# Where the SyncE queue issues the reload of the fourth expert's split weights

## The chip, the cores and the metric

One core of one Trainium2 chip runs the kernel. The metric is the device time of one launch in microseconds (us); where several runs are given, the median counts. Engines: TensorE (PE) multiplies matrices, VectorE (DVE), ScalarE (ACT) and GpSimd (POOL) do the rest, and SyncE (SP) issues most DMA transfers. "POOLq", "SPq" and so on are the instruction queues of these engines.

## The reference

The kernel computes a gated cross-attention layer and then a mixture of experts, on 32 sequences of 128 tokens of 256 values (4096 tokens).

```
x = x + tanh(g_xattn) * attention(layernorm(x), ctx, ctx)     # 16 heads of 16, causal
xf = layernorm(x)
logits = xf @ Wr + br                                          # 8 experts
keep the two largest, softmax over them -> weights
h = gelu(einsum('td,edh->eth', xf, W1) + b1)                   # 256 -> 1024, exact gelu
y = einsum('eth,ehd->etd', h, W2) + b2                         # 1024 -> 256
x = x + tanh(g_ffn) * sum over the kept experts of y * weights
```

## The kernel before

The program has two blocks, one after the other, each with its own instruction stream for every engine, and a barrier of all engines between them.

**The attention block** (`attention_and_routing`) runs a software pipeline over 16 groups of two sequences. Beside the attention it does three things for the experts. It splits each expert's W1 and W2 into a high and a low float16 part and stores them in DRAM (`split_weights`, `w_dram`), one layer of one expert with each group. It routes: for each token and each of its two experts POOL writes the token's normalised row into that expert's region of `token_rows` (`xs_dram`) with an indirect DMA (L471). And at its end (`padding`, L49) SP and ACT each write four blocks of padding rows behind the eight regions.

The on-chip tensor `wts` holds the split weights of all eight experts, 2 MB for each, but the attention block uses the places of experts 4 to 7 for its own operands. Hence the weights are loaded back from DRAM by `load_weights` (L56), two DMAs of 1 MB each for an expert. Experts 0, 1 and 2 are reloaded in the last groups of the attention's loop, expert 3 (`EARLY - 1`) after the padding, and experts 4 to 7 in the experts' block. Below, w3 is the reload of expert 3, w4 that of expert 4, and so on. Before each reload SP waits until the one before it has landed (`weights_in`), and SP's instructions behind such a wait have to wait with it.

**The block's end.** SP waits for its last stores, POOL for its last indirect DMAs, and then every engine goes through the barrier (L308; POOL's part of it begins with a DRAIN instruction). PE has no work there.

**The experts' block** (`experts`) runs over 39 tiles of 256 token rows, sorted by expert. For tile i, SP loads the rows `xs` (L1120, 272 KB), eight buffers deep; PE transposes them (L1276), multiplies by W1 (L1292) and by W2 (L1308); ACT applies gelu; DVE splits into two float16 parts; ACT scales by the routing weight; POOL adds the result to the output with an indirect DMA (L1168). Iteration `it(i)` of SP loads the rows of tile i + 2, and in its first iterations also the second layer's bias (`b2_all`, 1 MB) and weights: in `it(-1)` the bias and w4, in `it(0)` w5, in `it(1)` w6 and w7. On PE, `it(i)` transposes tile i + 2 first, then does layer 1 of tile i + 1, then layer 2 of tile i, strictly in this order, so PE stands still in `it(i)` until the rows of tile i + 2 have landed. Below, "row load j" is the load of tile j's rows, tiles counted from 0.

SP's queue is one queue in program order. The last lines of the attention block on it:

```python
                loop_over_groups(sp, it)
                padding(sp, env, range(E // 2))
                sp.wait_ge(weights_in, 16 * 2 * (EARLY - 1))
                load_weights(sp, wts, w_dram, EARLY - 1, weights_in)
```

The functions in full:

Of the kernel before, what the change touches and what calls it, by code (L numbers as in the profile page):

```python
# [19 lines left out]
E = 8  # L20
# [17 lines left out]
EARLY = 4  # L38
# [5 lines left out]
def padding(eng, env, experts):  # L44

    eng.wait_ge(env["pad_rows_ready"], 1)
    for e in experts:
        place = eng.value_load(env["padplace"][0:1, e:e + 1], min_val=0, max_val=E * REG)
        eng.dma_start(env["xs_dram"][bass.ds(place, TILE), :].rearrange("(h p) r -> p h r", h=2),  # L49
                      env["padrow"][:, :].unsqueeze(1).to_broadcast([P, 2, ROW])).then_inc(env["pads_in"], 16)  # L50


def load_weights(sp, wts, w_dram, e, done):

    for layer in range(2):
        sp.dma_start(wts[:, e, 4096 * layer:4096 * (layer + 1)], w_dram[e, layer]).then_inc(done, 16)  # L56
# [27 lines left out]
def there(g):  # L84

    return 0 <= g < NG if isinstance(g, int) else True
# [75 lines left out]
def attention_and_routing(nc, env):  # L162
# [11 lines left out]
    with ExitStack() as stack:  # L174
# [133 lines left out]
        with nc.Block() as block:  # L308

            @block.sync  # L310
            def _(sp):
# [85 lines left out]

                loop_over_groups(sp, it)
                padding(sp, env, range(E // 2))
                sp.wait_ge(weights_in, 16 * 2 * (EARLY - 1))  # L400
                load_weights(sp, wts, w_dram, EARLY - 1, weights_in)
                for i in range(2):
                    arrived(sp, x2_stored, NG - 2 + i, i)
                    settled(sp)
# [619 lines left out]
def experts(nc, env):  # L1024
# [8 lines left out]
    with ExitStack() as stack:  # L1033
# [30 lines left out]
        def settled(eng):  # L1064

            eng.sem_inc(waits_taken, 1)
# [15 lines left out]
        def all_tiles(eng, it):  # L1082


            pipeline(eng, it, 0, MAIN_TILES)
            ties = eng.value_load(mostint[0:1, 0:1], min_val=0, max_val=E)
            with eng.If(ties > 2):
                pipeline(eng, it, MAIN_TILES, ALL_TILES)

        def when(eng, ok, s, value):  # L1090

            if ok:
                eng.wait_ge(s, value)

        def before(i, n):

            return i >= n if isinstance(i, int) else True
# [4 lines left out]
        def added_value(i):  # L1102

            return i * 16 + 16

        with nc.Block() as block:

            @block.sync
            def _(sp):
                sp.wait_ge(rows_placed, 1)  # L1110
                sp.wait_ge(pads_in, 16 * E)

                def it(i, m, there):
                    if there(2):

                        j = i + 2
                        when(sp, before(j, RING), added[1], added_value(j - RING))
                        settled(sp)
                        row = sp.value_load(tile_row[0:1, bass.ds(j, 1)], min_val=0, max_val=E * REG)
                        sp.dma_start(xs[(m + 2) % RING][:, :, :],  # L1120
                                     xs_dram[bass.ds(row, TILE), :].rearrange("(h p) r -> p h r", h=2)
                                     ).then_inc(row_in[(m + 2) % RING], 16)
                    if isinstance(i, int) and i == -1:
                        sp.dma_start(b2_all[:, :, :].rearrange("p e d -> p (e d)"), b2.partition_broadcast(P)).then_inc(b2_in, 16)
                    if isinstance(i, int) and -1 <= i <= 1:

                        for e in {-1: (EARLY,), 0: (EARLY + 1,), 1: range(EARLY + 2, E)}[i]:
                            sp.wait_ge(weights_in, 16 * 2 * e)
                            load_weights(sp, wts, w_dram, e, weights_in)

                all_tiles(sp, it)
                sp.wait_ge(weights_in, 16 * 2 * E)
                sp.wait_ge(b2_in, 16)
# [221 lines left out]
```

## Time and profile before

| | us |
|---|---|
| median of three runs | 1036.77 |
| the three runs | 1031.41, 1036.77, 1039.24 |
| the profiled execution, whole | 1034.72 |
| its span, first to last instruction | 1033.0 |
| TensorE busy (matmul) in the span | 917.5 |
| TensorE's mean granted clock | 0.876 |

All rows of the trace count in us from the span's start. The profiled execution took 1.7 us more than its span. A clock of 1.0 is TensorE's upper level (2.4 GHz), 0.5 the lower (1.2 GHz).

### The profile page before, as it was taken

The page shows a single profiled execution, that of the slowest core. Times are in us where ns is not written, and L with a number is a line of the kernel's source. Part 1 is how long each engine was busy: PE and PEld are TensorE (multiplying, and loading weights), DVE is VectorE, ACT ScalarE, POOL GpSimd, SP SyncE. Part 2 cuts the span into 40 slices and gives each one's busy share as a digit, 9 for nine tenths or more (in the row PEclk, how much of TensorE's full clock was granted, in tenths as well). Part 3 has the DMA queues.
Part 4 walks back from the last instruction along what each step waited for, and adds up shares of the span by engine and source line. Part 5 has one row for each costly group of instructions (what it writes and reads, how often), then busy time and mean ns, then how long its engine had stood idle before and what let it go on. Part 6 is the DMA issues. An engine that isn't in the chain of part 4 may idle for free. (4 is left out here: it accounts for less than half of the span.)

```text
span 1033.0 us, 25346 instructions
## 1 busy us (share of the span) xinstructions
PE 917.5 (89%) x7545; PEld 814.6 (79%) x7601; DVE 628.4 (61%) x1521; ACT 444.1 (43%) x962; POOL 345.0 (33%) x355
## 2 busy tenths in 40 slices
PE   3799999999999999999951989999989989999991
PEld 2688888888888888888941879889879978989881
DVE  3467778777777787777453645565536554555650
ACT  2454444554444554344310544544535444544530
POOL 2222455433454533444321022323312331332222
PEclk9888888888888988887555999999989999999996
DMA  8855666656667566666258743323323332332221
GB/s 161 152 99 160 179 175 166 149 131 178 175 174 179 128 148 171 175 159 206 98 211 314 291 122 48 56 48 49 60 39 49 48 55 32 60 47 46 27 27 24
DMA packets 86072, 124.34 MB, mean 120 GB/s; under 512 B 8928, under 2 KB 77664, under 8 KB 81760
## 3 DMA queue, kind: packets, MB, share of 16 engines
q1 hardware_dynamic: 70592, 102.90, 37.7%
q0 software_dynamic: 14304, 19.15, 12.0%
q8 instruction: 57, 0.93, 0.4%
q10 hardware_dynamic: 1088, 1.11, 0.3%
q14 instruction: 31, 0.25, 0.1%
HBM read 55.21 MB, written 42.75 MB: 95 GB/s over the span
## 5 line engine op out<-in xcount | busy, mean ns | idle before, releaser
L1168 POOL DMA_INDIRECT out_rows<-yg,xs x78 | 126.1, 1617 | 352.4 <-ACT yg L1210 208.8
L1292 PE MATMUL bank<-xh,wts 128*128 128x256 f16 x1872 | 217.4, 278 | 0.0
L1308 PE MATMUL bank<-wts,hh 128*128 x1872 | 210.6, 273 | 0.0
L1292 PEld LDWEIGHTS bank<-xh,wts 128*128 x1872 | 186.6, 100 | 24.2
L1308 PEld LDWEIGHTS bank<-wts,hh 128*128 128x128 f16 x1872 | 183.2, 98 | 21.2
L454 POOL TENSOR_SCALAR_AFFINE_SELECT probs<-probs 128x512 f32<-128x512 f32 x128 | 95.8, 749 | 276.7 <-ACT probs L519 276.3
L1200 ACT ACTIVATE hf<-bank,b1t,gscale 128x256 f32<-128x256 f32 x312 | 154.8, 562 | 25.6 <-PE bank L1292 23.4
L909 PE MATMUL bank<-va,probs 128*128 128x17 f32 x1024 | 149.9, 281 | 9.9 <-DVE ao L631 9.8
L909 PEld LDWEIGHTS bank<-va,probs 128*128 128x128 f32 x1024 | 143.3, 216 | 14.5 <-DVE ao L631 12.2
L519 ACT ACTIVATE probs<-bank 128x512 f32<-128x512 f32 x128 | 76.4, 597 | 149.5 <-PE bank L894 148.4
L1210 ACT ACTIVATE yg<-yb,xs 128x256 f32<-128x256 f32 x78 | 35.4, 500 | 204.2 <-DVE yb L1249 188.2
L1239 DVE SCALAR_TENSOR_TENSOR hh<-hf,hscale,hh 128x512 f16<-128x512 f32 x156 | 117.3, 752 | 5.6
L681 DVE TENSOR_REDUCE rowmax<-bank 128x4 bf16<-128x512 f32 x128 | 87.8, 686 | 32.8 <-PE bank L833 20.4
L1249 DVE SCALAR_TENSOR_TENSOR yb<-bank,yscale,b_all 128x512 f32<-128x512 f32 x39 | 29.3, 751 | 107.4 <-PE bank L1308 107.4
L1238 DVE TENSOR_SCALAR hh<-hf,hscale 128x512 f16<-128x512 f32 x156 | 75.8, 486 | 26.6 <-ACT hf L1200 26.2
L471 POOL DMA_INDIRECT token_rows<-pay,slots x64 | 71.4, 1115 | 21.7 <-issue 11.1
L1223 DVE SCALAR_TENSOR_TENSOR xh<-bank,xh 128x512 f16<-128x512 f32 x39 | 27.0, 691 | 82.5 <-ACT xh L1191 82.5
L833 PEld LDWEIGHTS bank<-wts 96*128 96x128 bf16 x512 | 44.9, 108 | 23.2 <-issue 9.0
L833 PE MATMUL bank<-wts 96*128 96x128 bf16 x512 | 57.5, 242 | 5.6 <-issue 3.2
L891 PE MATMUL bank<-negident,rowmax 128*128 128x128 bf16 x512 | 55.8, 237 | 4.3 <-DVE rowmax L681 4.2
L1276 PE MATMUL bank<-ident,xs 128*128 128x128 f32 x156 | 25.5, 289 | 34.4 <-DMA xs<-token_rows 25.1
L894 PE MATMUL bank<-wts 96*128 96x128 bf16 x512 | 55.4, 236 | 0.0
(165 smaller groups left out, 1206.3 us busy)
## 6 DMA issues: line engine op xcount, KB each, us to landing
wts<-in_W SPq DMA_DIRECT2D x16, 1024.0 KB, 7.4
split_weights<-wts SPq DMA_DIRECT2D x16, 1024.0 KB, 4.9
wts<-split_weights SPq DMA_DIRECT2D x16, 1024.0 KB, 8.1
wts<-keys SPq DMA_DIRECT2D x96, 128.0 KB, 3.9
wts<-queries SPq DMA_DIRECT2D x96, 128.0 KB
xs<-token_rows SPq DMA_DIRECT2D x39, 272.0 KB, 2.8
xin<-in_x SPq DMA_DIRECT2D x16, 256.0 KB, 4.9
cin<-in_ctx_in SPq DMA_DIRECT2D x16, 256.0 KB, 6.1
```

Of the source, the lines that this page charges most:

```text
L454: pool.affine_select(out=probs[q % 4][:, :, :], in_=probs[q % 4][:, :, :], compare_op=ALU.is_ge, fill=0.0, base=0, pattern=[[0, 4], [1, P] ...
L471: pool.indirect_dma_start(out=xs_dram[:, :], out_offset=bass.IndirectOffsetOnAxis(ap=slots[par][:, b, r:r + 1], axis=0), in_=pay[par][:, b ...
L519: act.activation(probs[q % 4][:, :, :].rearrange("p a q -> p (a q)"), TB[q % 2][:, :], ACT.Exp, scale=float(DK) ** -0.5).then_inc(exp_read ...
L681: dve.tensor_reduce(rowmax[n % 2][:, :], SB[n % 2][:, :].rearrange("p (a k) -> p a k", a=4), AX, ALU.max).then_inc(max_ready, 1)
L833: last = pe.matmul(ps[:, i * P:(i + 1) * P], qst[par][:, 2 * j + odd, tok], kst[par][:, 2 * j + odd, tok], start=False, stop=i == 3)
L909: last = pe.matmul(OB[:, h * VA:(h + 1) * VA], probs[m % 4][:, a, :], va[i][:, b, h, :], start=True, stop=True)
L1168: pool.indirect_dma_start(out=out[:, :], out_offset=bass.IndirectOffsetOnAxis(ap=numbers, axis=0), in_=yg[m % 2][:, half, :], in_offset=No ...
L1200: last = act.activation(hf[:, c, :], HB[quarter][:, c % 2 * TILE:(c % 2 + 1) * TILE], ACT.Gelu, bias=b1t[:, bass.ds(e, 1), c], scale=gscal ...
L1238: step(dve.tensor_scalar(high, full, hscale[:, bass.ds(e, 1)], None, ALU.mult))
L1239: dve.scalar_tensor_tensor(out=hh[b][:, 1, c, :].rearrange("p c t -> p (c t)"), in0=full, scalar=hscale[:, bass.ds(e, 1)], in1=high, op0=A ...
L1292: last = pe.matmul(HB[c // 2][:, c % 2 * TILE:(c % 2 + 1) * TILE], wts[:, bass.ds(expert[1], 1), at:at + P], xh[b][:, xp, k, :], start=q = ...
L1308: last = pe.matmul(YB[b][:, half * D:(half + 1) * D], hh[b][:, hp, c, half * P:(half + 1) * P], wts[:, bass.ds(expert[0], 1), at:at + D], ...
```

## The change

w3 is no longer issued at the end of the attention block but in `it(-1)` of the experts' block, behind row loads 0 and 1 and the bias, where w4 was. w4 moves to `it(0)`, together with w5. w6 and w7 stay in `it(1)`. The waits on `weights_in` move with the loads. No transfer is added or left out.

```diff
--- before.py
+++ after.py
@@ -397,8 +397,6 @@
 
                 loop_over_groups(sp, it)
                 padding(sp, env, range(E // 2))
-                sp.wait_ge(weights_in, 16 * 2 * (EARLY - 1))
-                load_weights(sp, wts, w_dram, EARLY - 1, weights_in)
                 for i in range(2):
                     arrived(sp, x2_stored, NG - 2 + i, i)
                     settled(sp)
@@ -1124,7 +1122,7 @@
                         sp.dma_start(b2_all[:, :, :].rearrange("p e d -> p (e d)"), b2.partition_broadcast(P)).then_inc(b2_in, 16)
                     if isinstance(i, int) and -1 <= i <= 1:
 
-                        for e in {-1: (EARLY,), 0: (EARLY + 1,), 1: range(EARLY + 2, E)}[i]:
+                        for e in {-1: (EARLY - 1,), 0: (EARLY, EARLY + 1), 1: range(EARLY + 2, E)}[i]:
                             sp.wait_ge(weights_in, 16 * 2 * e)
                             load_weights(sp, wts, w_dram, e, weights_in)
```

On SP, the end of the attention block and the start of the experts' block, as one piece of the difference (`wts<-split_weights` is a weight load, `tile_row` the register load of a tile's address, `xs0` the buffer of row load 0):

```order
 L49 ISA
 L49 DMA token_rows<-padrow 128x2x272
-L56 DMA wts<-split_weights 128x4096 [waits weights_in]
-L56 DMA wts<-split_weights 128x4096
 L308 UNCONDITIONAL_BRANCH [waits x2_stored0,w_stored0,x2_stored1,w_stored1,params]
-L1108 UNCONDITIONAL_BRANCH [waits barrier_Pool_Activation_PE_DVE_SP_release]
-L1119 TENSOR_LOAD tile_row [waits rows_placed,pads_in]
```

The two DMAs of w3 are gone between the last padding and the block's end; the rows from L1108 on stand in the changed kernel too, with line numbers lower by two.

On SP in the experts' block, from row load 2 on, the kernel before (the first pair is w5, the second w6, the third w7):

```order
L1120 DMA xs2<-token_rows 128x2x272
L56 DMA wts<-split_weights 128x4096 [waits weights_in]
L56 DMA wts<-split_weights 128x4096
L1119 TENSOR_LOAD tile_row
L1119 ISA x2
L1120 ISA
L1120 DMA xs3<-token_rows 128x2x272
L56 DMA wts<-split_weights 128x4096 [waits weights_in]
L56 DMA wts<-split_weights 128x4096
L56 DMA wts<-split_weights 128x4096 [waits weights_in]
L56 DMA wts<-split_weights 128x4096
```

One pair of weight DMAs, with one wait, stood between row loads 2 and 3. The same stretch of the changed kernel (the pairs are w4, w5 and w6):

```order
L1118 DMA xs2<-token_rows 128x2x272
L56 DMA wts<-split_weights 128x4096 [waits weights_in]
L56 DMA wts<-split_weights 128x4096
L56 DMA wts<-split_weights 128x4096 [waits weights_in]
L56 DMA wts<-split_weights 128x4096
L1117 TENSOR_LOAD tile_row
L1117 ISA x2
L1118 ISA
L1118 DMA xs3<-token_rows 128x2x272
L56 DMA wts<-split_weights 128x4096 [waits weights_in]
L56 DMA wts<-split_weights 128x4096
```

Two pairs with two waits now stand between row loads 2 and 3. In front of row load 2 there is one pair in both kernels, and between row loads 3 and 4 two pairs in both.

## Rows read from the trace of the kernel before

**Rows 1.** The page: the span, and TensorE's granted clock in 40 slices

```profile
span 1033.0 us, 25346 instructions
...
PEclk9888888888888988887555999999989999999996
```

**Rows 2.** Timeline of SP's queue, 500 to 620: start, duration, line, operation, count

```profile
541.55 5.52 SPq L49 DMA_DIRECT2D token_rows<-padrow  x4
547.11 2.48 SPq L56 DMA_DIRECT2D wts<-split_weights  x2
560.10 1.63 SPq L1120 DMA_DIRECT2D xs<-token_rows  x2
...
562.28 0.91 SPq L56 DMA_DIRECT2D wts<-split_weights  x2
563.98 0.39 SPq L1120 DMA_DIRECT2D xs<-token_rows  x1
573.18 0.80 SPq L56 DMA_DIRECT2D wts<-split_weights  x2
574.79 0.39 SPq L1120 DMA_DIRECT2D xs<-token_rows  x1
580.40 9.41 SPq L56 DMA_DIRECT2D wts<-split_weights  x4
590.73 21.74 SPq L1120 DMA_DIRECT2D xs<-token_rows  x6
```

**Rows 3.** Timeline of PE, 545 to 620; in brackets the idle time before and its releaser

```profile
562.87 1.11 PE L1276 MATMUL bank<-ident,xs 128*128 128x128 f32 x4 [21.23 <-DMA xs<-token_rows]
...
573.90 0.66 PE L1276 MATMUL bank<-ident,xs 128*128 128x128 f32 x4 [0.92 <-DMA xs<-token_rows]
...
584.88 0.60 PE L1276 MATMUL bank<-ident,xs 128*128 128x128 f32 x4
...
590.55 5.40 PE L1308 MATMUL bank<-wts,hh 128*128 x48
598.92 0.66 PE L1276 MATMUL bank<-ident,xs 128*128 128x128 f32 x4 [2.96 <-DMA xs<-token_rows]
599.41 7.07 PE L1292 MATMUL bank<-xh,wts 128*128 128x256 f16 x48
```

**Rows 4.** Line L308, the barrier: count, duration min/median/max in ns, first and last start

```profile
L308 SPq DRAIN  x1: 13/13/13, 550.1 to 550.1; - x1
L308 POOLq DRAIN  x1: 5295/5295/5295, 552.8 to 552.8; - x1
```

**Rows 5.** Line L1106, the barrier at the kernel's end

```profile
L1106 POOLq DRAIN  x1: 4095/4095/4095, 1028.6 to 1028.6; - x1
```

**Rows 6.** Landing times of w3's two DMAs (issued at 547.1 and 548.5)

```profile
DMA to landing us min/median/max: 8.7/9.2/9.7
```

**Rows 7.** Packets of all DMA queues, 549 to 551, then 553 to 555

```profile
DMA packets 519, 0.71 MB, mean 354 GB/s; under 512 B 58, under 2 KB 456, under 8 KB 519
...
DMA packets 115, 0.86 MB, mean 428 GB/s; under 512 B 8, under 2 KB 11, under 8 KB 11
```

**Rows 8.** Landing of row load 3 (issued 574.79), then of row load 4 (590.73)

```profile
DMA to landing us min/median/max: 6.5/6.5/6.5
...
DMA to landing us min/median/max: 8.1/8.1/8.1
```

**Rows 9.** Waits of PE, 600 to 1033: total, times, longest

```profile
PE bank L1276 <- issue: 7.8, 2, 4.0
```

**Rows 10.** Timeline of PE at the first of these waits

```profile
757.69 1.11 PE L1276 MATMUL bank<-ident,xs 128*128 128x128 f32 x4 [3.86 <-issue]
758.60 7.75 PE L1292 MATMUL bank<-xh,wts 128*128 128x256 f16 x48
```

**Rows 11.** Windows 562.8:568.8 and 599.5:603: length, busy by engine, clock, DMA share, GB/s

```profile
562.80:568.80 6.00, 4.42 (x20) 3.32 (x21) 1.38 (x2) 1.20 (x2) 0.00 (x0) 0.50 1.00 382
...
599.50:603.00 3.50, 3.50 (x19) 2.43 (x18) 0.69 (x1) 1.40 (x3) 0.58 (x1) 0.51 0.16 31
```

## The prediction

> **What bounds the kernel now.** Start on the page with the span and the row of TensorE's clock [rows 1]: the clock lies at its lower level around the middle, where the two blocks meet. Then read the timeline of PE there [rows 3]. PE does nothing from about 541.6 to 562.87 (21.23 us) and then waits for row loads: 0.92 us in front of tile 2, nothing in front of tile 3, 2.96 us in front of tile 4. After that the list of PE's waits is nearly empty: 7.8 us in two pieces, both "issue" at a turn of the loop [rows 9], none for data. So from tile 4 to the end PE is the bound, nothing later has slack to lose or to take back, and the time is fixed by when PE can start tile 4. The tail behind PE's last product does not depend on the change.
>
> Two chains lead to tile 4. The first is the barrier, which sets when SP issues row load 0 (560.10). The second is SP's queue from there on.
>
> **The barrier.** Of the engines in the barrier SP is there at 550.1, POOL starts its DRAIN at 552.8 and holds it for 5.30 us, to 558.1 [rows 4]; SP's first row load follows 2.0 us later [rows 2]. POOL is last, and SP has 8 us to spare. So the 2.48 us in which SP issues w3 (547.11 to 549.59, rows 2) cost nothing today and give nothing back when they go: POOL's wait covers them. What can give something is the traffic of w3. It was queued on SP behind the padding: from 549 to 551 every one of 519 packets is under 8 KB, which the weight packets (4096 float16 of a partition, 8192 bytes) are not, and from 553 to 555 104 of 115 packets are 8 KB [rows 7]. w3 therefore hardly moves before POOL's last indirect DMAs have landed (552.8, where DRAIN begins), and moves during the whole DRAIN. The same DRAIN at the end of the kernel, with no other traffic, takes 4.10 us [rows 5]. Removing w3 from there is worth 0 if the DRAIN keeps its 5.30 us, and 5.30 - 4.10 = 1.2 us if the traffic makes the difference. An end further out: should the DRAIN wait for the queues to fall silent, it would end when the padding has landed, at about 553.3 (from 553 on hardly a small packet is left, rows 7), 4.8 us earlier. Against that speaks that it also takes 4.10 us in silence, and that w3's second DMA landed at 548.49 + 9.7 = 558.2 [rows 6], behind the DRAIN's end at 558.1. I take 1.2 us, the nearest pair of rows, with 0 and 4.8 as the ends.
>
> The Trainium skill (DMA: Bandwidth & Descriptors, "Queues, rings and completion order") says that each DMA engine goes round-robin over the queue rows that have work. By that rule w3 would have taken turns with POOL's DMAs from its issue at 547.1 on, and removing it would bring their landing forward by up to half of 552.8 - 547.1, some 2.8 us; the sum below would be +3.7 with it in place of +6.5. Rows 7 speak against it here, since w3 waited behind the padding in its own row of queues and only the padding took turns with POOL.
>
> **SP's queue in the experts' block.** Before, it runs like this [rows 2]: w4 at 562.28, row load 2 at 563.98; wait for w4; w5 at 573.18, row load 3 at 574.79; wait for w5; w6 at 580.40; wait for w6; w7 at 589.0 (the four DMAs from 580.40 end at 589.81, and a pair takes 0.80); row load 4 at 590.73. So the steps from one pair to the next are 10.9 us (with two row loads and the bias in the queue), 7.2 us and 8.6 us. A row load issued behind a pair goes through the same queue, and lands behind the pair: row load 3 took 6.5 us and row load 4 8.1 us [rows 8], where rows 0 and 1 reached PE 2.8 us after the first issue (560.10 to 562.87).
>
> After, counted from the same start of row load 0, every time before the shift by the barrier:
> - w3 at 562.28, row load 2 at 563.98. The queue holds what it held before, so row load 2 lands as before and tile 2 starts at 573.90.
> - w4 at 573.18 (10.9 us later, as w5 was). Then no row load, but the wait for w4: w5 at 580.40 (7.2 us).
> - row load 3 at 580.40 + 1.6 = 582.0 instead of 574.79. Its distance to the pair before it stays, and it was in place at 574.79 + 6.5 = 581.3, which is 8.1 us behind that pair. So now at 588.5. PE asked for tile 3 at 584.88 and did not wait. Now it waits 3.6 us.
> - w6 7.2 us behind w5, at 587.6. w7 8.6 us behind w6, at 596.2 (w6 again has a row load in front of it). Row load 4 at 597.9, in place 8.1 us later, at 606.0. It was in place at 598.8.
> - PE wants tile 4 11.1 us after tile 3 (584.88 to 590.55 + 5.40), at 599.6, and so waits 6.5 us in place of 2.96.
>
> Put shortly: row load 4 stood behind three waits for a landed pair (w4, w5, w6) and one unwaited pair (w7), now behind four (w3 to w6) and w7. One step more, **+7.2 us** at the start of tile 4. The 3.6 us at tile 3 lie inside it. Bounds: the cheapest of the three steps is 7.2, the next 8.6 us. Row loads 5 to 7 follow 1.2 to 1.6 us apart, and PE needs 11 us for a tile, so they are in time. w3 itself lands at about 573 and is not needed before the tiles of expert 3: 39 tiles over eight experts make that some 15 tiles of 11 us further on. No wait of PE for weights appears or is to be expected.
>
> **TensorE's clock.** The 2.96 us in front of tile 4 are followed by a stretch at 0.51 (599.5 to 603, rows 11), and layer 1 takes 7.07 in place of 5.40 us: 1.7 us lost. The wait of 3.86 us at 757.69 is followed by a layer 1 of 7.75 us [rows 10], with 0.5 us more on the transposes (1.11 against 0.60): 2.9 us lost. So a wait of 3 to 4 us costs 1.7 to 2.9 us in clock. Tile 4's wait becomes longer; its price rises by 0 to 1.2 us. I take 0.5. A fall behind the new wait at tile 3 costs nothing by itself: the work it slows has 6.5 us until row load 4 lands.
>
> **The sum.** 7.2 - 1.2 + 0.5 = +6.5 us. On the profiled execution 1034.72 + 6.5 = 1041.2. That execution lies 2.05 us under the median of the three runs, so on the median **1036.77 + 6.5 = 1043.3 us**, 0.6% slower. The bounds of the terms give +7.2 - 4.8 + 0 = +2.4 and +8.6 - 0 + 1.2 = +9.8, that is 1039.2 to 1046.6. What a measurement of this kernel can tell from no change is about 1%, 10.4 us; its three runs alone are 7.8 us apart.
>
> **Rivals.**
> - A, slower by over 1%: the clock falls at tile 3 and stays down over the second wait. For: when PE came back at 562.87 the clock was still at 0.50 until 568.8 [rows 11], 6 us. Then all work from 588.5 runs at half speed: the 11.1 us up to tile 4 become 22.2, tile 4 starts at 610.7 and not at 606.1 (+11.8 on 598.92), and if the level comes back 6 us after that, the half-speed stretch costs 3.0 us, 1.3 more than the 1.7 lost today. +11.8 + 1.3 - 1.2 = +11.9 us, 1048.7. It decides once the low stretch behind tile 3 is longer than 13 us, since it costs half its length and has the 6.5 us of slack to eat first; it passes 1% only if it lasts nearly to tile 4. Against: the wait of 3.86 us cost 2.9 us only. And the stretch of 6 us at 562.8 would itself end before 13. 0.12.
> - B, the barrier opens with silence and brings 4.8 us: 7.2 - 4.8 + 0.5 = +2.9, 1039.7. For: the DRAIN's end and w3's landing lie 0.1 us apart. A smaller form of it is that w3 took turns with POOL's last DMAs and held them up by up to half of 5.7 us: 7.2 - 2.8 + 0.5 - 1.2 = +3.7, 1040.5. 0.15 for both.
> - C, row loads do not queue behind a pair but land as in a quiet queue after 2.8 us. Then row load 3 is there at 584.8, in time, row load 4 at 600.7, 1.9 us later than before, and the sum is 1.9 - 1.2 = +0.7, 1037.5. Against: 6.5 and 8.1 us [rows 8]. 0.05. Together with B it would be the one way to a gain, of 2.9 us, still not 1%.
> - That the change doesn't do what it says: the order of SP's instructions shows it done, and only a start of tile 4 set by something else would hide it. The row of PE says it waited for row load 4 [rows 3]. Inside C.
>
> My forecast has 0.68. Run-to-run scatter of a few us lies over all of them and carries a part of the forecast's upper end, and of A, over the line of 1%. Faster by over 1% 0.02, within 1% 0.84, slower by over 1% 0.14. The range: from just above C's place, which is left out, through B to the upper bound with A and the scatter: 1037.5 to 1049.5.
>
> **What the profile after would show.** POOL's DRAIN at L308 near 4.1 us and row load 0 about 1.2 us earlier (558.9); in SP's queue one pair between row loads 1 and 2 and two between 2 and 3, with 7 us between them; a wait of PE for `xs` of about 3.6 us at tile 3, where there was none, and of 6.5 us at tile 4; no wait for weights; the rest of the experts' block unchanged in length. What would make it wrong: a DRAIN that ends with the traffic (B), a landing of row load 3 before 585 (C), or a clock row with a longer low stretch around 589 to 612 (A).

## The result and the profile after

The change makes the kernel slower by 0.7%: ratio to before 1.0068, 95% interval 1.0043 to 1.0093. The medians of twelve runs each are 1042.75 us after and 1036.54 before. Forecast were +6.5 us (0.6%) and 1043.3 us. The profiled execution took 1040.65 us, its span 1038.9.

SP's queue after, the timeline from 500 to 625 (columns as in [rows 2], with which this is to be compared):

```profile
541.04 5.36 SPq L49 DMA_DIRECT2D token_rows<-padrow  x4
558.86 1.63 SPq L1118 DMA_DIRECT2D xs<-token_rows  x2
560.54 0.47 SPq L1122 DMA_DIRECT2D b_all<-in_b  x1
561.05 0.91 SPq L56 DMA_DIRECT2D wts<-split_weights  x2
562.76 0.39 SPq L1118 DMA_DIRECT2D xs<-token_rows  x1
572.59 8.08 SPq L56 DMA_DIRECT2D wts<-split_weights  x4
581.47 0.39 SPq L1118 DMA_DIRECT2D xs<-token_rows  x1
587.50 9.18 SPq L56 DMA_DIRECT2D wts<-split_weights  x4
597.49 18.27 SPq L1118 DMA_DIRECT2D xs<-token_rows  x6
```

Subtract the start of row load 0 in each: row load 3 is issued 22.6 us behind it (before 14.7), row load 4 38.6 us (before 30.6). The row "572.59 ... x4" is the new pair of pairs, w4 and w5, in front of row load 3. PE's timeline after, 555 to 620, answers to [rows 3]:

```profile
573.31 0.66 PE L1274 MATMUL bank<-ident,xs 128*128 128x128 f32 x4 [0.99 <-DMA xs<-token_rows]
...
588.26 0.66 PE L1274 MATMUL bank<-ident,xs 128*128 128x128 f32 x4 [3.81 <-DMA xs<-token_rows]
588.75 7.07 PE L1290 MATMUL bank<-xh,wts 128*128 128x256 f16 x48
595.66 5.40 PE L1306 MATMUL bank<-wts,hh 128*128 x48
605.13 0.66 PE L1274 MATMUL bank<-ident,xs 128*128 128x128 f32 x4 [4.07 <-DMA xs<-token_rows]
605.62 7.07 PE L1290 MATMUL bank<-xh,wts 128*128 128x256 f16 x48
```

Tile 3 now waits 3.81 us where there was no wait. Tile 4 waits 4.07 in place of 2.96, and starts 46.3 us after row load 0 is issued; before it was 598.92 - 560.10 = 38.8. The wait is 2.4 us shorter than the forecast's 6.5 us. 1.7 us of that is layer 1 behind tile 3, which took 7.07 us and not 5.40: the low clock there used up slack that the forecast had counted as waiting. The rest is that tile 3 started 1.0 us later than forecast (29.4 us behind row load 0, not 28.4), and tile 4 0.3 us later. After tile 4 PE waits for nothing but the two turns of the loop, as in [rows 9].

The two barriers, lines L308 and L1104 (L1106 before), answer to [rows 4] and [rows 5]:

```profile
L308 SPq DRAIN  x1: 7/7/7, 546.9 to 546.9; - x1
...
L308 POOLq DRAIN  x1: 5295/5295/5295, 551.5 to 551.5; - x1
```

```profile
L1104 POOLq DRAIN  x1: 4094/4094/4094, 1034.6 to 1034.6; - x1
```

POOL's DRAIN has the same 5295 ns to the nanosecond. It only starts earlier in relation to what goes before. The difference of the spans, 5.9 us, adds up: the padding was issued 541.55 - 541.04 = 0.5 us earlier (the attention block of this execution), from there to row load 0 it took 17.8 us in place of 18.55 (-0.7), tile 4 starts 7.45 us later in relation to row load 0, and from tile 4 to POOL's last DRAIN it took 429.5 us in place of 429.7 (-0.2). In sum +6.0.

### The profile page after: what moved, and what is told of

It reads as the page before. It is cut to its first block and busy times, and to the rows that moved or that the text cites. A ratio compares the mean times of both kernels' runs of the same rounds, so it can differ in the third digit from the quotient of the medians.

```text
span 1038.9 us, 25346 instructions
## 1 busy us (share of the span) xinstructions
PE 921.7 (89%) x7545; PEld 817.5 (79%) x7601; DVE 627.8 (60%) x1521; ACT 444.1 (43%) x962; POOL 346.4 (33%) x355
## 3 DMA queue, kind: packets, MB, share of 16 engines
q10 hardware_dynamic: 1088, 1.11, 0.3%
## 5 line engine op out<-in xcount | busy, mean ns | idle before, releaser
L1274 PE MATMUL bank<-ident,xs 128*128 128x128 f32 x156 | 25.6, 290 | 38.6 <-DMA xs<-token_rows 29.5
```

## The experiments

Two theories. **Q:** the number of pairs in SP's queue in front of row load 4, each with a wait for its landing, sets the start of tile 4, and PE carries that delay to the end. **R:** what costs is the new wait in front of tile 3, with the low clock behind it. Ratios are to the kernel before on the same chip. Two times are read from every trace: from row load 0's issue to the start of tile 4, and from POOL's last indirect DMA (L471) to its DRAIN.

**e1, one pair in front of row load 3, three in front of row load 4.**

```diff
-for e in {-1: (EARLY - 1,), 0: (EARLY, EARLY + 1), 1: range(EARLY + 2, E)}[i]:
+for e in {-1: (EARLY - 1,), 0: (EARLY,), 1: range(EARLY + 1, E)}[i]:
```

> The changed kernel with w4 alone in it(0) and w5, w6, w7 in it(1): one pair of weight DMAs between row loads 2 and 3, as before, but three between row loads 3 and 4, so that row load 4 still stands behind w3 to w7. Theory Q (the number of pairs in SP's queue in front of row load 4 sets the start of tile 4, and with it the end): PE does not wait in front of tile 3 any more, waits some 6 to 8 us in front of tile 4, which starts 46 us after row load 0 is issued, as in the changed kernel (46.3), against 38.8 in the kernel before; the time is that of the changed kernel within 2 us, a ratio to before of 1.005 to 1.008. Rival R (the new wait in front of tile 3, 3.8 us with the low clock behind it, is what costs): with that wait gone some 5 us come back, ratio 1.000 to 1.002.

Measured: 1.0078, 1.005 to 1.0106. PE's timeline of this kernel, 582 to 620:

```profile
584.49 0.60 PE L1274 MATMUL bank<-ident,xs 128*128 128x128 f32 x4
584.93 5.40 PE L1290 MATMUL bank<-xh,wts 128*128 128x256 f16 x48
590.17 5.40 PE L1306 MATMUL bank<-wts,hh 128*128 x48
605.74 1.11 PE L1274 MATMUL bank<-ident,xs 128*128 128x128 f32 x4 [10.17 <-DMA xs<-token_rows]
606.65 7.07 PE L1290 MATMUL bank<-xh,wts 128*128 128x256 f16 x48
```

The wait in front of tile 3 is gone, and has gone over to tile 4, which starts 605.74 - 559.66 = 46.1 us after row load 0. R is wrong: no time came back, and its ratio of 1.000 to 1.002 lies outside the interval. The wait at tile 3 is only an advance on the one at tile 4. One number of the expectation was off: PE waits 10.17 us for tile 4 and not 6 to 8, since without a wait at tile 3 it is ready the earlier.

**e2, the barrier's part alone** (w3 behind row load 7, the rest as before). Left out below: the condition around the loop also takes in `i == 5`, SP's waits in it count w3 as the last pair, and PE waits once, in it(7), for all weights.

```diff
-                sp.wait_ge(weights_in, 16 * 2 * (EARLY - 1))
-                load_weights(sp, wts, w_dram, EARLY - 1, weights_in)
...
-for e in {-1: (EARLY,), 0: (EARLY + 1,), 1: range(EARLY + 2, E)}[i]:
+for e in {-1: (EARLY,), 0: (EARLY + 1,), 1: range(EARLY + 2, E), 5: (EARLY - 1,)}[i]:
```

> The barrier's part alone: the kernel before, but w3 is taken out of the end of the attention block and issued behind row load 7 (in it(5)), where no row load that PE waits for stands behind it; w4 to w7 stay where they were, and PE waits once, in it(7), for all weights. Theory Q: the barrier brings what it brought between the two profiles (0.7 us from the last padding's issue to row load 0), tile 4 starts 38.8 us after row load 0 as before; time -0.7 us, ratio 0.998 to 1.000. Rival (the traffic of w3 held up the barrier for 1.2 us or more, as the forecast took it): -1.2 to -4.8 us, ratio 0.995 to 0.999, with a DRAIN on POOL shorter than 5.3 us. A ratio over 1.002 would say that the place behind row load 7 costs something.

Measured: 0.9987, 0.9967 to 1.0007, which fits both sizes. The trace says more: DRAIN 5295 ns, 17.8 us from the first padding to row load 0 (before 18.55). Tile 4 starts 37.5 us after row load 0, 1.3 earlier than in the first trace of before, after a wait of 1.73 us, and its layer 1 takes 5.40 us. The rival's shorter DRAIN did not come.

**e3, the suspected cost doubled** (w2 moved too).

```diff
-if isinstance(g, int) and NG - 2 <= g <= NG:
+if isinstance(g, int) and NG - 2 <= g <= NG - 1:
...
-for e in {-1: (EARLY - 1,), 0: (EARLY, EARLY + 1), 1: range(EARLY + 2, E)}[i]:
+for e in {-1: (EARLY - 2,), 0: (EARLY - 1, EARLY, EARLY + 1), 1: range(EARLY + 2, E)}[i]:
```

The first pair of lines takes w2's reload out of the attention's loop.

> The suspected cost doubled: the changed kernel, and w2 too is taken out of the attention block; it(-1) issues w2, it(0) w3, w4 and w5, it(1) w6 and w7. Row load 3 stands behind four pairs in place of two (before) and three (changed), row load 4 behind six. Theory Q: each further pair is one more step of 7.2 to 8.6 us, so tile 4 starts 53.5 to 55 us after row load 0; the attention block may end some tenths of a us earlier; time +13 to +16 us on before, ratio 1.012 to 1.016. Rival R (the cost is the one wait at tile 3 and its low clock): PE's wait at tile 3 becomes about 11 us but that at tile 4 none, and the time rises by less than one step over the changed kernel, ratio 1.007 to 1.011. A low clock over the whole of it would give over 1.018.

Measured: 1.0101, 1.0069 to 1.0132. SP's timeline and PE's timeline of this kernel:

```profile
560.18 1.64 SPq L1118 DMA_DIRECT2D xs<-token_rows  x2
...
573.08 15.45 SPq L56 DMA_DIRECT2D wts<-split_weights  x6
589.34 0.39 SPq L1118 DMA_DIRECT2D xs<-token_rows  x1
595.75 8.50 SPq L56 DMA_DIRECT2D wts<-split_weights  x4
605.06 31.06 SPq L1118 DMA_DIRECT2D xs<-token_rows  x7
```

```profile
596.58 1.11 PE L1274 MATMUL bank<-ident,xs 128*128 128x128 f32 x4 [11.61 <-DMA xs<-token_rows]
597.48 7.38 PE L1290 MATMUL bank<-xh,wts 128*128 128x256 f16 x48
...
612.41 0.66 PE L1274 MATMUL bank<-ident,xs 128*128 128x128 f32 x4 [2.31 <-DMA xs<-token_rows]
612.90 5.40 PE L1290 MATMUL bank<-xh,wts 128*128 128x256 f16 x48
```

Tile 4 starts 52.2 us after row load 0, one step of 6.0 us more than in the changed kernel. Q had 53.5 to 55 us, with a step of 7.2 to 8.6, and a ratio of 1.012 to 1.016, so both came out under it. Beside the shorter step two gains were not in it: the stretch from the first padding to row load 0 fell to 16.55 us (-2.0 on before), and layer 1 of tile 4, behind a wait of 2.31 us, took 5.40 and not 7.07 us (-1.7). 13.4 - 2.0 - 1.7 = +9.7 us, measured 1.01% of 1036, 10.5 us. R's range of ratios held the number, but not its mechanism: there is a wait at tile 4 also.

**e5, no pair in front of the row loads** (the kernel before, w4 to w7 behind row load 7).

```diff
-if isinstance(i, int) and -1 <= i <= 1:
+if isinstance(i, int) and i == 5:
-for e in {-1: (EARLY,), 0: (EARLY + 1,), 1: range(EARLY + 2, E)}[i]:
+for e in range(EARLY, E):
```

> The kernel before with w4 to w7 all issued in it(5), behind row load 7, and w3 left at the end of the attention block: no weight pair stands in front of a row load that PE needs soon (the bias still does). Theory Q: row loads 2 to 7 land within about 3 to 10 us behind row load 0, PE waits for no row load from tile 2 on; gone are the waits of 0.9 and 3.0 us and the 1.7 us of low clock behind the second: -4 to -6 us, ratio 0.994 to 0.996. Rival (the time to tile 4 is bound by PE's own work at the low clock, and the waits are only its slack): no change, ratio 0.999 to 1.001.

Measured: 0.9939, 0.9918 to 0.9961, 6.3 us faster than before, a little more than Q's 4 to 6. Row load 4 is issued 5.3 us after row load 0; PE's timeline has no wait at tiles 2, 3 and 4, and tile 4 starts 34.8 us after row load 0 (560.40):

```profile
595.23 0.60 PE L1276 MATMUL bank<-ident,xs 128*128 128x128 f32 x4
```

The rival, that these waits are only PE's slack, is wrong.

**e4 and e7, the same with w3, then with w2 and w3, taken along.** In e4 the changed kernel issues `range(EARLY - 1, E)` at `i == 5`, in e7 `range(EARLY - 2, E)`, and w2 goes from the attention block as in e3.

> The changed kernel with w3 to w7 all issued in it(5), behind row load 7. It joins the barrier's part (0.7 us, as the traces of e1 and e2 repeated it) to what e5 gained. Theory Q: tile 4 starts 34.8 us after row load 0 as in e5, no wait of PE for a row load from tile 2 on, time e5 minus 0.7, so -6 to -7.5 us on before, ratio 0.993 to 0.994. Rival (the barrier's 0.7 us is only scatter between executions): equal to e5, 0.994.

> As e4, and w2 too is taken out of the attention block and issued first in it(5). In e3 the stretch from the first padding to row load 0 was 16.55 us with w2 gone, against 17.8 with w3 gone and 18.4 to 18.6 with both there. If that is w2's traffic in front of POOL's last indirect DMAs, 1.2 us more are gained here: -7.5 to -9 us on before, ratio 0.9915 to 0.993. If it was scatter: as e4.

Measured: e4 0.9958 (0.9942 to 0.9975), e7 0.9953 (0.9934 to 0.9972). The traces have the gains at the barrier (from first padding to row load 0 17.9 us in e4, 17.2 in e7), and tile 4 at 35.0 and 35.5 us, but the times do not show them: both are at or above e5, whose interval overlaps. I expected more from both. (e5 ran on another chip than e4 and e7; each ratio is to the kernel before on its own chip.) What the experiments can tell is that all weights behind row load 7 is 0.4 to 0.6% faster than before and, from the ratios to before, 1.1 to 1.3% faster than the changed kernel; where w2 and w3 stand besides is under what they resolve.

**e9, the same order without SP's waits** (the edit is to the changed kernel).

```diff
-                            sp.wait_ge(weights_in, 16 * 2 * e)
                             load_weights(sp, wts, w_dram, e, weights_in)
...
+                        if isinstance(i, int) and i == 7:
+                            pe.wait_ge(weights_in, 16 * 2 * E)
                         pe.wait_ge(weights_in, expert[1] * (16 * 2) + 16 * 2)
```

> The changed kernel, its order of DMAs on SP unchanged (w3 in it(-1), w4 and w5 in it(0), w6 and w7 in it(1)), but without SP's waits between the pairs; PE waits once, in it(7), for all weights instead. It tells apart what a step in front of row load 4 consists of. Theory W (a step of 7.2 to 8.6 us is 5.1 us of data, 2.1 MB at some 410 GB/s, and 2 to 3.5 us in which the queue stands empty while SP waits for the landing and issues again): all pairs are issued at once, the queue never runs empty, row load 3 lands about 21 us after row load 0 is issued and row load 4 about 32, both before PE needs them (24 and 35), no wait in front of tiles 3 and 4: as e5, ratio 0.993 to 0.996. Rival D (the data in front of row load 4 is what counts, waits or none): tile 4 starts more than 42 us after row load 0, ratio over 1.003.

Measured: 0.9964, 0.9946 to 0.9982; tile 4 starts 595.16 - 558.83 = 36.3 us after row load 0, without a wait, and tile 3 without one too:

```profile
595.16 0.66 PE L1273 MATMUL bank<-ident,xs 128*128 128x128 f32 x4
```

The data in front of row load 4 are those of the changed kernel. The busy share of the DMA engines (in tenths, 40 slices) and the GB/s from 564 to 590, first of the changed kernel, then of e9:

```profile
DMA  9999999999510091699999940485999999780938
GB/s 416 403 429 429 429 403 466 429 400 332 189 60 15 12 202 25 277 454 454 441 416 416 403 164 0 63 139 239 441 429 416 403 479 403 314 314 15 113 101 340
```

```profile
DMA  9999999999999999999999999999999999999999
GB/s 429 391 466 416 429 441 403 441 388 357 426 428 427 457 416 429 429 416 416 416 416 429 403 441 430 362 382 398 431 404 403 441 416 441 416 403 416 416 429 403
```

With the waits the DMA engines stand empty between the pairs; without them they never do. Row load 4 is issued at 571.24, 12.4 us after row load 0 (38.6 in the changed kernel). So a step is 2.1 MB of data at 410 to 430 GB/s, some 5 us, and 2 to 3 us of empty queue from the wait for its landing. Rival D is wrong: tile 4 starts 10 us earlier with the same data in front of its rows. But the data count too. Row loads 3 and 4 landed 25.0 and 36.3 us after row load 0, later than the 21 and 32 that W had, so row load 4 came just as PE was ready for it: one more pair in front of it, 5 us of data, would by this reckoning have made PE wait. The ratio is a little above W's 0.996.

**e6 and e8, what the barrier gains.**

```diff
                 padding(act, env, range(E // 2, E))
+                for layer in range(2):
+                    act.dma_start(env["spare"][layer], w_dram[0, layer]).then_inc(env["spare_in"], 16)
```

> The kernel before, with two additional DMAs of 1 MB each from DRAM to DRAM issued by ACT behind its padding, so that the DMA queues are busy for about 5 us longer, past the end of POOL's DRAIN. What is looked at is the DRAIN at L308 alone. If the DRAIN has a length of its own (5.30 us in all six traces so far, with and without w3's traffic), it stays at 5.30. If traffic or the last landing sets it, it becomes longer by 1 us or more, up to 10 us. Row load 0 waits for more in either case, since POOL's last indirect DMAs land later.

Measured, in one execution (1038.34 us; the barrier is line L310 there):

```profile
L310 POOLq DRAIN  x1: 5295/5295/5295, 557.1 to 557.1; - x1
```

The DRAIN is as long with 2.3 MB moving during it (here) as with w3 moving through all of it (before) and with queues silent but for its first 0.6 us (the changed kernel), so traffic does not set it. That leaves the time in front of it:

```diff
                 padding(sp, env, range(E // 2))
+                sp.wait_ge(env["pads_in"], 16 * E)
                 sp.wait_ge(weights_in, 16 * 2 * (EARLY - 1))
                 load_weights(sp, wts, w_dram, EARLY - 1, weights_in)
```

> The kernel before, with one more wait on SP in front of w3, until all eight padding blocks have landed, so that w3 is in no DMA queue while POOL's last indirect DMAs land; it then moves during POOL's DRAIN, within SP's spare time. Looked at is the time from POOL's last indirect DMA at L471 to the start of its DRAIN: 7.0 us with w3 queued (before), 6.3 us with w3 gone (the changed kernel). Theory H (w3 already delays these landings while it stands in SP's queue behind the padding): 6.3 us here, DRAIN 5.30. Rival S (the 0.7 us has another cause, as the shorter instruction stream of the block): 7.0 us here. Row load 0 may be late, since w3 may still be moving then.

> The kernel before once more, unchanged, on the same chip, as the measure of how much the time from POOL's last indirect DMA to its DRAIN scatters: 6.98 us in the first profile. Theory H and rival S both expect 6.8 to 7.1 us; 6.3 us here would mean that the 0.7 us between the kernels is scatter.

> The changed kernel once more, unchanged, on the same chip: 6.1 to 6.4 us from POOL's last indirect DMA to its DRAIN (6.10 in its first profile), DRAIN 5.30, tile 4 46 us after row load 0 is issued.

Measured: POOL's last indirect DMA and its DRAIN in e8 (timeline of POOL, then line L308):

```profile
547.87 0.97 POOL L472 DMA_INDIRECT token_rows<-pay,slots  x1 [0.30 <-issue]
```

```profile
L308 POOLq DRAIN  x1: 5295/5295/5295, 554.2 to 554.2; - x1
```

554.2 - 547.9 = 6.3 us. The kernel before, a second time:

```profile
545.97 0.97 POOL L471 DMA_INDIRECT token_rows<-pay,slots  x1 [0.31 <-issue]
```

```profile
L308 POOLq DRAIN  x1: 5295/5295/5295, 552.9 to 552.9; - x1
```

That is 6.9 us. Over all traces: 6.9 to 7.0 us with w3 queued behind the padding (before twice, e5, e6), 6.3 us with w3 elsewhere or later (changed kernel twice, e1, e2, e4, e8, e9; the last expectation has 6.10 us for the changed kernel's first trace, in which it is 6.3), 5.0 and 5.7 us with w2 gone too (e3, e7). Theory H holds for the size, 0.6 to 0.7 us, and rival S is wrong. Row load 0 was not late in e8: it came 17.9 us after the first padding, as in the changed kernel.

The packets tell what is late. In all of these traces but e3 and e7 the last packet of POOL's queue ends 5.5 us after the start of its last indirect DMA, whether w3 is queued or not. In the kernel before that is 551.3, and w3's first packet of 8 KB starts only at 552.2. What comes later with w3 queued is the signal of the landing: POOL's wait for it ends 1.1 to 1.3 us behind that last packet, and 0.6 us behind it with w3 elsewhere. In e3 and e7 it is the packets themselves that end earlier, 4.3 and 4.9 us after that start.

The single times were 1032.99 us for e8, 1034.38 for the kernel before and 1042.92 for the changed one. In the second pair of traces tile 4 starts 38.85 and 45.80 us after row load 0, 6.95 us apart (7.45 in the first pair).

## Why the prediction was right

**PE as the bound, and tile 4 as the point that fixes the end:** right. From tile 4 to the end both kernels take the same. In the changed kernel, e1, e3 and e5 the measured time agrees with the sum from the trace (tile 4, barrier, clock) within 1.2 us; in e2, e4, e7 and e9 1 to 2.4 us less were gained than their one trace adds up to (e4: -3.8 - 0.6 - 1.7 = -6.1, measured -4.4 with -6.0 to -2.6), which is at the edge of what their intervals allow. The traces show where single executions differ beside these terms: the first padding is issued at 540.9 us in one and at 546.6 in another (the changed kernel's two traces: 541.0 and 543.9), though up to there only e3 and e7 differ from the kernel before, while from tile 5 to POOL's last DRAIN all thirteen traces take 415.9 to 417.4 us. So the sums of single traces cannot be trusted to 1 or 2 us.

**The term of 7.2 us:** right in mechanism and size, 7.45 and 6.95 us in two pairs of traces. e1 showed that the count in front of row load 4 matters and not where the pairs stand before it, e3 that one more step adds 6.0 us, which is under the 7.2 that I had as the cheapest. What the forecast took as given, that a step is 7.2 us and not the 5 us of its data, e9 took apart.

**The barrier, -1.2 us:** the sign was right and the size wrong, -0.7, and the reason behind the size fell. The step was the comparison of two DRAINs, 5.30 and 4.10 us, as one with traffic and one without. The DRAIN at this barrier is 5.295 us in every trace, with and without traffic. The 4.10 at the end belongs to that place. I had left this as the end "0 if the DRAIN keeps its 5.30 us", without seeing that the part in front of the DRAIN could shrink. What shrank is the time until POOL sees its last indirect DMAs landed. The Trainium skill (DMA: Bandwidth & Descriptors, "Queues, rings and completion order") says that each DMA engine goes round-robin over the queue rows that have work; the estimate that the prediction made with it was up to 2.8 us. The direction is as measured, but turns between packets are not the cause of the 0.7 us: w3's packets start 0.9 us or more after POOL's last one has ended, and POOL's packets end no earlier with w3 gone. How a DMA that waits in its queue delays the signal of another queue's landing by 0.6 us stays open; only that it does is shown, by e8. That this term had the right sign is luck: the forecast expected it from the DRAIN, and it came from in front of the DRAIN.

**The clock, +0.5 us:** measured 0.0 in both pairs: layer 1 of tile 4 took 7.07 us in both kernels. Its wait was 3.9 to 4.1 us and not 6.5, and no run has one of 6.5. In e1, behind 10.17 us, layer 1 took 7.07 us too, and the four transposes 1.11 in place of 0.66. The fall behind tile 3 cost nothing by itself, as forecast: its 1.7 us went into the slack in front of tile 4. Windows of the changed kernel at the two falls (columns as in [rows 11]):

```profile
589.20:592.60 3.40, 3.40 (x19) 2.42 (x17) 0.89 (x2) 1.37 (x3) 0.00 (x0) 0.50 0.93 369
606.30:609.70 3.40, 3.40 (x19) 2.40 (x17) 1.27 (x3) 1.14 (x3) 0.60 (x1) 0.50 0.71 141
```

**The rivals:** A (clock down over both waits) did not come; the falls are 3.4 us each. B (a barrier that opens with silence) fell with the DRAIN's fixed length, and its smaller form (turns between w3 and POOL's DMAs) with the packets above. C (row loads that do not queue) fell with the waits of PE. The sum by what was measured is 7.45 - 0.7 + 0.0 = +6.7 us; the runs say +7.0 (4.5 to 9.6).

## What to carry to other kernels

Count, for each small load that an engine will wait for, how many large transfers with a wait for their landing stand in front of it in the same queue; each costs its data time and the empty queue behind it (here 5 us and 2 to 3 us). A large load that is wanted late belongs behind all the small ones that are wanted soon: all weights behind the eight row loads was faster than either order by 0.4 to 1.3%. Where the waits between the large loads can go, that helps nearly as much: e9 kept the order of the changed kernel and came out 1.0% under it by the ratios to before. Moving work out of a barrier gives nothing by itself if another engine is the last at it; look for what that last engine waits for.

## What the runs showed of the hardware

- POOL's DRAIN at the block's barrier took 5295 ns in all thirteen traces, with the DMA queues full or silent; at the kernel's end it took 4094 or 4095 ns.
- A reload of 2 MB that stood in SP's queue behind other DMAs, and of which no packet moved from 549 to 551, still made POOL wait 0.6 to 0.7 us longer for its indirect DMAs (6.9 to 7.0 us from the last one to the DRAIN, 6.3 without it), though the last packet of POOL's queue ended 5.5 us after that DMA's start either way.
- Five pairs of weight loads of 2 MB, issued without waits between them, landed 5.1 to 5.7 us apart (e9); with a wait for the landing before each next pair 7.2 to 8.2 us apart (the changed kernel, second trace).
- PE's waits of 1.71 us (e6), 1.73 us (e2), 2.13 us (e8) and 2.31 us (e3) were followed by a layer 1 of 5.40 us; after those of 2.46 us (before, second trace) to 4.07 us it took 7.07 us each time, with the granted clock at its lower level (1.2 GHz) for 3.4 us.
